# Attention, shared FFN, routing and scatter of an audio-tower layer as one pipeline of 16 groups, with expert regions of 4096 rows

## What is computed

```python
h = signature(x) @ W.T + b                  # depth 4 over 8 channels, scanned over the steps
a = layernorm(h)
q, k, v = batchnorm(a@Wq+bq), softmax_t(a@Wk+bk), batchnorm(a@Wv+bv)   # 8 heads, DK = 16
lam_c = einsum('bkt,bvt->bkv', k, v)        # one 16x16 matrix for each batch
lam_p = relu(conv3x3(v, Wpos))              # over (DK, time)
Y = einsum('bhkt,bkv->bhvt', q, lam_c) + einsum('bhkt,bkvt->bhvt', q, lam_p)
h = h + Y @ Wout + bout
a = layernorm(h)                            # then top-1 of 8 experts, weight 1
e = argmax(a @ gate_w.T)
h = h + (silu(a@w1[e].T) * (a@w3[e].T)) @ w2[e].T + gelu(a@sw1.T) @ sw2.T
```

## Time and profile before

| | us |
|---|---|
| time, median of 3 runs | 863.74 (863.05 to 865.87) |
| span of the profiled execution, first to last instruction | 856.8 |
| what lies around the span, to the median | 6.9 |
| PE busy in it | 735.9 (86%) |
| DVE busy | 542.9 (63%) |
| POOL busy | 294.7 (34%) |
| ACT busy | 273.2 (32%) |
| mean granted clock of TensorE, as a share of 2.4 GHz | 0.915 |

### The profile page before, as it was taken

One profiled execution on the slowest core, in us unless ns is written; L12 is line 12 of the kernel. 1 busy time (PEld: TensorE's weight loads), 2 busy tenths in 40 slices (PEclk: granted clock), 3 DMA queues, 4 the chain that ended last, 5 costly groups with the idle time before them and its releaser, 6 DMA issues. The chain is left out here.

```text
span 856.8 us, 14895 instructions
## 1 busy us (share of the span) xinstructions
PE 735.9 (86%) x3950; PEld 598.7 (70%) x3951; DVE 542.9 (63%) x1395; ACT 273.2 (32%) x586; POOL 294.7 (34%) x366
## 2 busy tenths in 40 slices
PE   2799999999999999529999999997656969988882
PEld 1587777777777778327878777776655957877772
DVE  8777777666777777536866757854724846655551
ACT  3122222222222222023443434433414834434340
POOL 5210100010011010015655646633473025666663
PEclk9999999999999999756998989999666979999996
DMA  9100000000000000221121112110642531112110
GB/s 294 30 11 15 14 14 14 14 14 14 14 17 14 17 14 14 60 75 67 55 69 58 64 57 67 64 48 19 177 123 77 160 86 43 49 50 54 50 33 8
DMA packets 55995, 45.71 MB, mean 53 GB/s; under 512 B 23848, under 2 KB 50450, under 8 KB 55394
## 3 DMA queue, kind: packets, MB, share of 16 engines
q1 hardware_dynamic: 51778, 38.60, 16.5%
q0 software_dynamic: 4192, 6.81, 2.8%
HBM read 31.57 MB, written 14.78 MB: 54 GB/s over the span
## 5 line engine op out<-in xcount | busy, mean ns | idle before, releaser
L304 POOL TENSOR_TENSOR TOP<-A2T,Vhalf 126x512 f32 (+1 forms) x32 | 36.1, 1129 | 257.0 <-PE PS L530 254.4
L674 POOL TENSOR_TENSOR Pl<-PF,Ph 128x512 fp32r<-128x512 f32 x64 | 80.8, 1282 | 53.2 <-ACT Ph L740 53.1
L493 PE MATMUL PS<-Wh,Ah 128*126 128x512 f32 (+1 forms) x320 | 89.7, 410 | 5.3 <-issue 3.0
L493 PE MATMUL PS<-Wh,Al 128*126 128x512 f32 (+1 forms) x320 | 85.5, 397 | 0.0
L842 DVE SCALAR_TENSOR_TENSOR P<-PS,QN 128x512 f32<-128x512 f32 x64 | 43.8, 685 | 65.3 <-PE PS L937 62.0
L493 PE MATMUL PS<-Wl,Ah 128*126 128x512 f32 (+1 forms) x320 | 84.9, 395 | 0.0
L395 DVE SCALAR_TENSOR_TENSOR Z<-PS,Vt,Z 126x128 f32<-126x128 f32 x224 | 78.3, 350 | 7.2 <-PE PS L493 0.4
L944 PE MATMUL PS<-P,K 128*128 128x256 f32 x256 | 72.3, 432 | 0.0
L493 PEld LDWEIGHTS PS<-Wh,Al 128*126 128x126 f32 (+1 forms) x320 | 59.9, 187 | 15.1
L493 PEld LDWEIGHTS PS<-Wl,Ah 128*126 128x126 f32 (+1 forms) x320 | 59.8, 187 | 14.5
L328 ACT ACTIVATE AS<-PS 128x504 f32<-128x504 f32 x32 | 18.9, 591 | 151.7 <-PE PS L522 151.7
(11 more groups left out here) (226 smaller groups left out, 1728.2 us busy)
## 6 DMA issues: line engine op xcount, KB each, us to landing
IM<-v_pad SPq DMA_DIRECT2D x64, 164.2 KB
WR<-in_w SPq DMA_DIRECT2D x8, 512.0 KB
routed<-nobody SPq DMA_DIRECT2D x1, 2574.0 KB, 14.7
XS<-routed SPq DMA_DIRECT2D x39, 66.0 KB
x_rows<-XR SPq DMA_DIRECT2D x16, 129.9 KB
WR<-in_w SPq DMA_DIRECT2D x8, 256.0 KB
q_raw<-QS SPq DMA_DIRECT2D x32, 63.0 KB
QR<-q_raw SPq DMA_DIRECT2D x32, 63.0 KB, 1.9
```

What stands on the lines that cost most here:

```text
L304: pool.tensor_tensor(TOP[:, 1 - u].rearrange("p (a b) -> p a b", b=C), A2T[:, bass.ds(t, 1)].rearrange("p t a b -> p (t a b)").unsqueeze(2 ...
L493: ins = pe.matmul(psU[u][h].rearrange("p d o -> p (d o)"), a[0:rows, u, c], w[0:rows, c, h], start=(n == 0 and c == 0), stop=(n == 2 and c ...
L674: pool.tensor_tensor(Pl[:, u, b], PF[:, b], Ph[:, u, b].bitcast(f32), ALU.subtract).then_inc(pl_ready, 1)
```

## The change

- `attention` and `shared` become one function `middle`: a pipeline over 16 groups, written out with no hardware loop. In step k it works on the convolution of group k, on the output product, layer norm, gate and first FFN product of group k-1 (`g`), on the second FFN product of group k-2 (`f`), and GpSimd scatters the rows of group k-4.
- The products over the key axis are all f32 and not split: `Ph`, `Pl` and `BD` are gone. Each is a product with 32 columns of weights, whose result goes to 32 of the 128 partitions of `psY` (`j` picks them). The convolution takes two batches at once, one in partitions 0 to 35 and one in 64 to 99.
- `LC` has the order (batch, value, head), is still made by VectorE from PSUM; queries are loaded group by group.
- Every expert has a region of 4096 rows in `routed`, so a place needs only the counts so far (`RUN`), not the totals. Rows carry normalized values, token number and residual sum (260 numbers), and `base`, `x_rows` and the gather of `BG` are gone. `routed` is filled with "nobody" rows, 34,560 rows in 30 transfers, during `signatures`.
- `signatures` also loads and splits the first expert weights (`w1_high`, `w1_low`), and GpSimd makes `HB` (`H` plus the output bias) for each tile, which is stored in `h_rows`; `H` has two buffers in place of 32.
- `experts` is written out, loads `XS` from a row number read from a table `RO` into 8 buffers, and GpSimd only scatters.

```diff
+                if on(k - 1, 0, NT):
+                    pool.wait_ge(h_ready, k)
+                    if isinstance(k, int):
+                        if k >= 3:
+                            pool.wait_ge(h_stored[1 - u], 16 * ((k - 1) // 2))
+                    else:
+                        pool.wait_ge(h_stored[1 - u], freed[u])
+                    pool.tensor_tensor(HB[:, 1 - u], H[:, 1 - u], boutb[:], ALU.add).then_inc(hb_ready, 1)
...
-                    ht = H[:, bass.ds(t, 1)].rearrange("p t c -> p (t c)")
+                    wait_from_one(dve, hb_ready, k - 2)
+                    ht = H[:, w]
                     dve.tensor_tensor(ht, psH, tokb[:], ALU.add).then_inc(h_ready, 1)
...
+                    sp.wait_ge(hb_ready, t + 1)
+                    sp.dma_start(h_rows[bass.ds(t * TOK, TOK), HC - IDC:ROW - IDC], HB[:, u]).then_inc(h_stored[u], 16)
+                    if on(k - 2, 0, FILLS):
+                        sp.dma_start(routed[bass.ds(t * FILL * 128, FILL * 128), :].rearrange("(t p) c -> p t c", p=128),
+                                     nobody[:].unsqueeze(1).broadcast_to([128, FILL, ROW])).then_inc(routed_set, 16)
...
+            def w1_low(j, u):
+                pool.wait_ge(w1_hi, (j - 3) * 2 + u + 1)
+                pool.tensor_tensor(W1l[:, bass.ds(j - 3, 1), I * u:I * u + I].rearrange("p e i -> p (e i)"), WRW[:, u],
+                                   W1h[:, bass.ds(j - 3, 1), I * u:I * u + I].rearrange("p e i -> p (e i)").bitcast(f32),
+                                   ALU.subtract).then_inc(w1_lo, 1)
...
+            def gelu(g, h):
+                act.wait_ge(up_done, 2 * g + h + 1)
+                wait_from_one(act, down_done, g)
+                act.activation(Gh[:, 2 * h:2 * h + 2], psU[h], ACT.Gelu).then_inc(gh_ready, 1)
+                act.activation(GF[:, 2 * h:2 * h + 2], psU[h], ACT.Gelu).then_inc(gf_ready, 1)
...
+            def products(g, q):
+                h, pair = q // 2, q % 2
+                dve.wait_ge(conv_done, 4 * g + q + 1)
+                for hb in range(2):
+                    b = 2 * hb + pair
+                    ins = dve.scalar_tensor_tensor(P[:, b, HV * h:HV * h + HV], psC[2 * pair + hb], 0.0,
+                                                   QN[:, g % 2, b:b + 1].broadcast_to([128, HV, SP]), ALU.max, ALU.mult)
+                ins.then_inc(p_ready, 1)
...
+            def place(m):
+                dve.wait_ge(rank_done, m + 1)
+                L.link(dve.tensor_tensor(RK[:], psR, OH[:, m % 2], ALU.mult))
+                L.link(dve.tensor_reduce(posf[:], RK[:], AX.X, ALU.add))
+                dve.tensor_copy(POS[:, 4 * m:4 * m + 4], posf[:]).then_inc(pos_ready, 1)
...
+            def conv(g, q):
+                h, pair = q // 2, q % 2
+                wait_from_one(pe, p_ready, 4 * g + q - 1)
+                if q == 0:
+                    pe.wait_ge(im_in[g % 2], 128 * (g // 2 + 1))
+                for hb in range(2):
+                    r = 64 * hb
+                    ins = pe.matmul(PS[2 * pair + hb][:, :], W36[r:r + 36], IM[r:r + 36, g % 2, VB * pair + HALF * h:VB * pair + HALF * h + HALF],
+                                    start=True, stop=True)
+                ins.then_inc(conv_done, 1)
+            def add_products(g, h):
+                pe.wait_ge(p_ready, 4 * g + 2 * h + 2)
+                for r in (2 * h, 2 * h + 1):
+                    for j in range(4):
+                        ins = pe.matmul(psY[32 * j:32 * j + 32], K[:, K_BD + 24 - 8 * r:K_BD + 56 - 8 * r], P[:, :, 4 * r + j],
+                                        start=False, stop=(r == 3))
+                ins.then_inc(sum_done, 1)
...
+                pe.matmul(psR, K[0:TOK, K_LR:K_LR + TOK], oh, start=True, stop=False)
+                for t in range(3):
+                    pe.matmul(psR[:, t + 1:4], ones, oh[:, t:t + 1].broadcast_to([TOK, 3 - t, E]), start=False, stop=False)
+                pe.matmul(psR, ones, RUN[:, m:m + 1].broadcast_to([TOK, 4, E]), start=False, stop=True).then_inc(rank_done, 1)
...
+            for k in range(SLOTS):
+                if k >= XB:
+                    n = k - XB
+                    sp.wait_ge(stored[n % 2], 16 * (n // 2 + 1))
+                r = sp.value_load(RO[0:1, k:k + 1], min_val=0, max_val=(FILL * FILLS - 1) * 128)
+                sp.dma_start(XS[:, k % XB], routed[bass.ds(r, 128), :]).then_inc(xs_in[k % XB], 16)
...
+            for k in range(SLOTS):
+                pool.wait_ge(os_ready, k + 1)
+                pool.indirect_dma_start(out_rows, bass.IndirectOffsetOnAxis(XS[:, k % XB, IDC:IDC + 1].bitcast(i32), 0), OS[:, k % 2], None,
+                                        bounds_check=N - 1, oob_is_err=False).then_inc(stored[k % 2], 16)
```

The step of each engine in `middle`, PE's first:

```diff
+            def step(k):
+                w, f, g = (k + 1) % 2, k - 2, k - 1
+                if on(k, 0, NG):
+                    conv(k, 1)
+                if on(g, 0, NG):
+                    add_products(g, 1)
+                if on(k, 0, NG):
+                    conv(k, 2)
+                if on(g, 0, NG):
+                    pe.wait_ge(yc_ready, g + 1)
+                    pe.wait_ge(lc_ready, min(k + 1, NG))
+                    if k == NG:
+                        pe.wait_ge(pos_ready, (k - 4) // 2 + 1)
+                    for t in range(2):
+                        ins = pe.matmul(psH[:, t], YC[:, g % 2, 2 * t:2 * t + 2].rearrange("p b s -> p (b s)"), WO[:], start=True, stop=True)
+                    ins.then_inc(ht_done, 1)
+                if on(f, 0, NG):
+                    down(f)
+                if on(k, 0, NG):
+                    conv(k, 3)
+                    pe.wait_ge(lc_ready, k + 1)
+                    pe.wait_ge(qn_ready, k + 1)
+                    wait_from_one(pe, yc_ready, k)
+                    wait_from_one(pe, bs_ready, k - 1)
+                    for b in range(GB):
+                        ins = pe.matmul(psY[:, b], LC[:, k % 2, DK * b:DK * b + DK].rearrange("p v h -> p (v h)"), QN[:, k % 2, b],
+                                        start=(b == 0), stop=False)
+                    ins.then_inc(yc_done, 1)
+                if on(g, 0, NG):
+                    pe.wait_ge(xn_ready, g + 1)
+                    for t in range(2):
+                        ins = pe.transpose(psX[:, TOK * t:TOK * t + TOK], R[:, g % RB, t, 0:F], ident_t)
+                    ins.then_inc(xt_done, 1)
+                if on(k, 0, NG):
+                    add_products(k, 0)
+                if on(g, 0, NG):
+                    pe.wait_ge(xg_ready, 2 * g + 2)
+                    for t in range(2):
+                        ins = pe.matmul(psG[:, t], XG[:, g % 2, TOK * t:TOK * t + TOK], GW[:], start=True, stop=True)
+                    ins.then_inc(gate_done, 1)
+                    up(g)
+                if k % 2 and on((k - 3) // 2, 0, NM):
+                    if on(g, 0, NG):
+                        pe.wait_ge(lg_ready, g + 1)
+                    rank((k - 3) // 2)
+                if on(k + 1, 0, NG):
+                    pe.wait_ge(kh_ready, k + 2)
+                    if on(g, 0, NG):
+                        pe.wait_ge(lg_ready, g + 1)
+                    if k % 2 and k >= 3:
+                        pe.wait_ge(pos_ready, (k - 3) // 2 + 1)
+                    for b in range(GB):
+                        ins = pe.matmul(psL[:, b], KH[:, w, b].rearrange("p h k -> p (h k)"), VT[:, (k + 1) * GB + b].rearrange("p j r -> p (j r)"), start=True, stop=True)
+                    ins.then_inc(lam_done, 1)
+                    conv(k + 1, 0)
...
+            def step(k):
+                w, f, g = (k + 1) % 2, k - 2, k - 1
+                if on(f, 0, NG):
+                    gelu(f, 1)
+                if on(g, 0, NG):
+                    act.wait_ge(sum_done, 2 * g + 2)
+                    wait_from_one(act, ht_done, g - 1)
+                    act.activation(YC[:, g % 2], psY[:, :, 0:S], ACT.Copy).then_inc(yc_ready, 1)
+                if on(k + 1, 0, NG):
+                    wait_from_one(act, lam_done, k)
+                    act.activation(KH[:, w], KT[:, (k + 1) * GB:(k + 2) * GB].unsqueeze(2).broadcast_to([S, GB, NH, DK]),
+                                   ACT.Copy).then_inc(kh_ready, 1)
+                if on(k - 2, 0, E):
+                    e = k - 2
+                    act.wait_ge(w2_in[e % 2], 16 * (e // 2 + 1))
+                    act.activation(W2[:, e, :, 0], WR2[:, e % 2], ACT.Copy).then_inc(w2_hi, 1)
+                if on(g, 0, NG):
+                    act.wait_ge(mv_ready, 2 * (g + 1))
+                    act.activation(SD[:, g % 2, :, 0], MV[:, g % 2, :, 1], ACT.Sqrt, bias=eps[0:TOK, :]).then_inc(sd_ready, 1)
+                    act.wait_ge(xt_done, g + 1)
+                    wait_from_one(act, gate_done, g - 1)
+                    wait_from_one(act, xl_ready, g - 1)
+                    wait_from_one(act, up_done, 2 * (g - 1))
+                    act.activation(X2h[:, g % 2], psX, ACT.Copy).then_inc(xg_ready, 1)
```

(42 more changed lines are left out.)

1009 lines of the change are left out of this document (333 added, 676 removed).

## The result

The changed kernel takes **926.98 us** (921.67 to 930.24, 4 runs) against 863.39 us (861.93 to 865.87, 4 runs) for the kernel before in the same comparison: a ratio, worked out over the runs, of **1.070, 95% interval 1.063 to 1.077** (the two medians alone give 1.074). It is slower, as forecast, by 64 us where 31 were forecast. Its profiled execution took 926.16 us and has a span of 924.3.

The account below looks back on a forecast made before the run. PE was taken as the signature stage's bound, GpSimd as the experts' pace. Span 856.8 + 97 (signatures) - 46 (middle) - 16 (experts) = 892, with 6.9 around it 899, rounded down to 895 us; range 830 to 980.

Parts of the forecast that it names:

- Signature stage: Signature stage: closed loop of waits in each tile plus lost clock, +97 us, from +60 to +135.
- The chain: Signature tile: PE's psH, VectorE's H, GpSimd's HB, then TOP; PE stands 2.8 us, net 2.4 a tile, +72 us.
- half of the tiles: Signature stage: clock falls after the idle stretch, half of 30 tiles lose 1.7 us each, +25, between 0 and +50.
- Middle: Attention and shared FFN merged: 294 us against 340, so -46, between -105 and +15; a step 15.0 us.
- ten small operations for two groups: Middle step, VectorE: routing adds ten small operations for two groups, each at most 0.26 us, 1.0 us a group.
- the clock term: Middle step: PE works about 10 of 14 us, clock some 0.8, adding 0.7 us to 14.3, so 15.0.
- Side by side at a quarter: Middle, sums over the key axis: four 32-column products run together, 1.8 us a group against 7.2 one after another.
- the rival: Middle: 32-column products run one after another, +5.4 us a group less 1 idle, +70, so 965 us; chance 0.19.
- Table loads: Middle, ScalarE: two 1.28 us loads a step counted as hidden; rival uncovered, +41 us, 936, chance 0.06.
- `LC` at nothing: Middle, VectorE: LC's new order, still one 512-element pass from PSUM, costs nothing, at worst twice 0.7 us a group.
- Code runs dry: Rival, middle and experts: PE at half pace in written-out code for a fifth of 300 us, +50, 945; chance 0.17.
- Experts: Experts: GpSimd no longer binds, PE does, slots 3.3 us in place of 3.68; -16 us, between -35 and 0.

Follow-up runs that it names:

- the version of the three edits: Changed kernel with TOP ahead of HB, routing operations moved around LC, and scatters between QN and X2l: 755.39 us, 0.905 of the kernel before.
- the kernel with the wait alone: Kernel before, with GpSimd waiting for H of tile k-1 ahead of TOP of tile k+1, no HB made: 935.95 us, 1.116 of the kernel before.

## Why the prediction came out as it did

The direction and its cause were right; the size was half of what came. The terms were off by +11 for the signatures, +40 for the middle and -19 for the experts, +32 in all, so one error partly hid another.

**Signature stage: +108, forecast +97.** The chain was right. GpSimd was to start 0.28 us after `H`'s end and started 246.90 - 246.72 = 0.18 after it; `HB` took 0.45 (0.44 forecast) and `TOP` 1.07; PE stood 2.34 to 2.5 us in place of 2.8, 74.3 in all where 80 were forecast. The wait for `XN` went, as it should. The mis-sized term is the clock: I let half of the tiles lose 1.7 us, 0.85 on the mean. In the changed kernel every tile from the third on lost, and 13.79 - 10.34 - (2.4 - 0.4) = 1.45. So +25 measured some +45, of a range that ended at 50. I had also misread: a mean of 0.55 from 608 to 609 puts the fall at 608.1, which is 2.1 us behind PE's last matmul and not 2.6. The idle stretch that I forecast was clearly longer than that, and "half of the tiles" had no ground. "Near 430" for the last half product was too early as well; it is 454.4.

**Middle: -6, forecast -46.** This is the part that failed. The start took 28 us (31 forecast), the sixteen steps 274 or 17.1 each (240 and 15.0), the end 32 (23). (The 17.8 above is the mean of the thirteen steps in the middle.) The step that failed is "ten small operations for two groups, each at most `H`'s 0.26: 1.0 a group". The ten took 2.4 us a group (half the sum of their means). That bound came from an operation that reads PSUM while GpSimd was idle. These read SBUF beside GpSimd's passes, and the two longest took 2.7 and 3.0. With it went the clock term: I added 0.7 a step for a clock of 0.8 and for "about 10 of 14 us" of PE work. The clock was 0.72, and PE is busy 160.6 us in thirteen steps, 12.4 each, even in the version of the three edits, at 0.89.

I had rows that show the hold: `Vt` with eight elements at 664 ns beside `TOP` in the kernel before, which I named as "held up by `TOP`", and then did not carry over to the new operations. "SBUF — State Buffer" of the Trainium skill, under "SBUF: two separate sides", states it as a rule: VectorE and GpSimd share a pair of ports as an exclusive lock, and whichever operation starts first keeps it for its whole length, where VectorE's has two inputs in SBUF or runs in a two-port mode. The trace agrees on which operations are held: beside the same pass of `QN`, `OH`, with two such inputs, took 0.54 us until that pass ended, while `top`, a reduction of one input, took 0.19. On who goes first it does not simply agree: `eq`'s recorded start is 0.22 us before that of the first `Gl`, and `eq` was still held until the second had ended.

It also explains a gain that I missed. The normalization of the rows, 941 ns in the kernel before, takes 343 now; before, it was 339 to 345 too where no pass of GpSimd lay beside it. With the routing operations moved the step is 14.96 (14.6 over fifteen steps from start to start), near the forecast's 15.0. That agreement is partly luck, since I had left out the gain and counted 0.4 for the scatters. The end is 9 us longer than forecast. Its last scatter is issued at 789.9, the first rows for the experts are asked for at 797.05, and PE waits 13.4 us for them.

**Side by side at a quarter: right.** Two calls of 1.07 us are 2.1 a group, where I took 1.8, and in one set of columns they take 3.6 or more each. By the factor that "TensorE: Matmul & The Clock Gate" of the Trainium skill gives in its Part 3 the cost would have been 3.0; the measured factor, for four sets, is 3.4. The price of the rival was +70 and is +30 to +33. PE's longer work fills its idle time and keeps the clock up: in that run PE is idle 26 of 302 us in the middle at a clock of 0.92, in the changed kernel's steps 51 of 274 at 0.72.

**Table loads and `LC` at nothing: right.** With no loads in the loop nothing changes. `LC` is one pass of 692 ns. The rule of the Trainium skill that the prediction names, to batch calls by table set, would have given 41 us here, and no run shows any of it.

**Code runs dry: not seen.** PE is busy 115.4 of 119 us in the experts, all of it code written out. The stall that this rival was built on, 14.5 of 31 us, is itself missing on one of the chips where the kernel before takes 838 us, with the same code.

**Experts: -35, forecast -16.** GpSimd did cease to bind. PE's slot is (907.2 - 799.1) / 38 = 2.84 us and not 3.3. I had taken PE's shortest distance in the earlier trace rows for its work, but the row itself shows an idle 0.16 to 0.65 ahead of the first matmul of a slot, time in which PE waited for others: an upper bound that I used as a value.

## What to carry to other kernels

When an operation is put ahead of another on an engine, ask what it waits for, and whether the bound engine gives that only in the same round: a wait with no work in it cost 98 us here, and turning two operations round gave 121 back. Add the clock to every wait that comes back each round: here it nearly doubled the price. On VectorE, price a small operation by what GpSimd does at that moment and not by its size, and put those that read SBUF where GpSimd is idle. A wait that names a VectorE operation is only half read until that operation's own duration has been looked at.

## What the runs showed of the hardware

- VectorE's operations on 4 to 32 elements in SBUF took 0.17 to 0.22 us alone, mostly 0.4 to 1.2 beside a pass of GpSimd and up to 3.01 beside two passes in a row of 1.25 each. Reductions of one input kept their 0.19, and the `P` passes, with one input in PSUM, their 0.68.
- f32 products on 32 columns ran at 0.067 us an instruction over four sets of columns and at 0.23 in one, and the order among the sets did not matter.
- PE idle for 2.4 us in each tile was followed by some 3 us at a clock of 0.50, in every tile from the third; idle for 1.9 to 2.0, the same in all but two of the tiles behind the third, and those two were 1.5 us shorter. A stall of 2.0 us cost 3.1.
- The kernel before took 838 us in two comparisons and 863 to 865 in three, the changed one 924 to 927 beside both. In the kernel with the wait alone, on a chip of the first kind, PE did not stall in the shared FFN while GpSimd scattered (29.9 of 30 us busy, against 14.5 of 31). What makes the stall stays open.
